# A routing stage in straight code, with four input slots and the matrix products made one and two steps ahead

## What is computed

```
scores = softmax(xf @ gate_w)                        # 8 experts
_, sel = top_k(scores + expert_bias, 2)              # two experts per token
# routed tokens, scaled by their scores, are gathered by expert (sorted by expert number);
# every token also passes the shared expert:
shared = (silu(xf @ sw1) * (xf @ sw3)) @ sw2         # hidden width 224
x = layernorm(x + routed + shared)
```

## Time and profile before

| | us |
|---|---|
| median of 3 runs | 2471.24 |
| lowest and highest | 2467.26, 2482.78 |
| the profiled execution, device time | 2470.14 |
| its span (first to last instruction) | 2468.5 |
| the stage, its start to the start of the next phase | 163.1 |
| granted TensorE clock over the whole span (share of 2.4 GHz) | 0.942 |

### The profile page before, as it was taken

The page is one execution under the profiler, slowest core; times in us unless marked ns, Lnnn a source line. Parts: engine busy times, 40 slices in busy tenths (PEclk is TensorE's granted clock), DMA queues, the critical chain, the costliest instruction groups (busy, mean ns, idle before and its releaser), DMA issues. The chain is left out here.

```text
span 2468.5 us, 60390 instructions
## 1 busy us (share of the span) xinstructions
PE 2021.4 (82%) x19761; PEld 1508.3 (61%) x19761; DVE 1871.6 (76%) x4879; ACT 1552.7 (63%) x2923; POOL 1541.1 (62%) x2367
## 2 busy tenths in 40 slices
PE   8965888888788888888887599888499967878998
PEld 5643655556556556656555488766355535658997
DVE  4546999999999999999999544456433328976886
ACT  5657999999999999999998122255222212333443
POOL 2346888998888999899999323234211125635666
PEclk9986999999999999999999699988699989998999
DMA  5776677766776767676765458544322224531111
GB/s 166 240 219 162 180 188 186 179 185 183 182 191 181 184 183 178 180 195 180 191 183 148 115 161 243 166 143 149 97 81 84 85 75 141 152 94 60 51 56 38
DMA packets 295157, 373.66 MB, mean 151 GB/s; under 512 B 44628, under 2 KB 234647, under 8 KB 294903
## 3 DMA queue, kind: packets, MB, share of 16 engines
q1 hardware_dynamic: 284710, 342.05, 50.2%
q0 software_dynamic: 9872, 27.28, 3.5%
q10 hardware_dynamic: 320, 1.05, 0.2%
HBM read 151.03 MB, written 85.00 MB: 96 GB/s over the span
## 5 line engine op out<-in xcount | busy, mean ns | idle before, releaser
L760 PE MATMUL p_ps_sc<-p_CR,p_BR 64*128 64x128 f32 x4096 | 310.6, 292 | 149.7 <-DVE p_M L1061 91.0
L674 POOL TENSOR_TENSOR p_CR<-p_pc 128x256 f32<-128x256 f32 x512 | 375.2, 733 | 65.3 <-DVE p_pc L1044 52.8
L678 POOL TENSOR_TENSOR p_BR<-p_pb 128x256 f32<-128x256 f32 x512 | 375.2, 733 | 31.0 <-DVE p_pb L1053 13.4
L760 PEld LDWEIGHTS p_ps_sc<-p_CR,p_BR 64*128 64x128 f32 x4096 | 265.2, 194 | 207.3 <-issue 149.9
L906 ACT ACTIVATE p_D<-p_ps_x 128x512 f32<-128x512 f32 x512 | 289.4, 592 | 71.4 <-PE p_ps_x L726 70.0
L1061 DVE TENSOR_TENSOR p_M<-p_ps_sc,p_D 128x1024 f32<-128x1024 f32 x256 | 309.7, 1210 | 6.5 <-issue 3.5
L1044 DVE SCALAR_TENSOR_TENSOR p_pc<-p_ps_c,p_beta,p_cs 128x256 f32<-128x256 f32 x512 | 241.6, 472 | 34.8 <-DMA p_sn<-p_tr_s 17.3
L775 PE MATMUL p_ps_y<-p_M,p_uexp 128*32 128x128 f32 x4096 | 259.8, 282 | 0.0
L1044 DVE SCALAR_TENSOR_TENSOR p_pc<-p_ps_c,p_beta,p_sn 128x256 f32<-128x256 f32 x512 | 241.2, 471 | 0.0
L1053 DVE SCALAR_TENSOR_TENSOR p_pb<-p_ps_b,p_beta,p_cs 128x256 f32<-128x256 f32 x512 | 241.2, 471 | 0.0
L1053 DVE SCALAR_TENSOR_TENSOR p_pb<-p_ps_b,p_beta,p_sn 128x256 f32<-128x256 f32 x512 | 241.2, 471 | 0.0
(11 more groups left out here) (285 smaller groups left out, 5096.3 us busy)
## 6 DMA issues: line engine op xcount, KB each, us to landing
p_cs<-p_tr_c SPq DMA_DIRECT2D x256, 256.0 KB
p_sn<-p_tr_s SPq DMA_DIRECT2D x252, 256.0 KB
p_phib<-scratch_phi SPq DMA_DIRECT2D x256, 128.0 KB
p_x<-scratch_rt SPq DMA_DIRECT2D x72, 128.0 KB, 2.0
scratch_ro<-p_o POOLq DMA_DIRECT2D x72, 128.0 KB, 2.0
p_xT<-in_xT SPq DMA_DIRECT2D x64, 128.0 KB, 4.3
scratch_u<-p_u SPq DMA_DIRECT2D x16, 512.0 KB, 3.6
scratch_wu<-p_wu SPq DMA_DIRECT2D x16, 512.0 KB, 4.3
```

Source lines behind the costliest of these rows:

```text
L674: e.tensor_tensor(CR[:, p, g, :], pc[:, g % 2, 0, :], pc[:, g % 2, 1, :], ALU.add).then_inc(S["rotC"], 1)
L678: e.tensor_tensor(BR[:, p, g, :], pb[:, g % 2, 0, :], pb[:, g % 2, 1, :], ALU.add).then_inc(S["rotB"], 1)
L760: m = e.matmul(sc_ps[half][:, (g * 2 + b) * L:(g * 2 + b + 1) * L], BR[half * 64:half * 64 + 64, p, 2 * q + g, b * L:(b + 1) * L], CR[half ...
```

## The change

The stage is rewritten in its order, in its buffers and in its form; no instruction of the computation itself is added or removed.

- Slots: x1 and x1T have four slots (NX) in place of two, with a semaphore for each slot and tensor. SP's first loads fill four slots; in the steps it does `store(t)`, then `load(t+4)`, x1T before x1. x1T waits only for `b_mm` (steps t and before), x1 for `xr_ok` and `rows_ok`.
- PE: g_ps, a_ps and b_ps exist twice (8 banks in all in place of 5). `gate` runs two steps ahead and `up` one: gate(0), gate(1), up(0), then per step up(t+1), gate(t+2), rank(t), down(t).
- ACT: silu(t), scale_rows(t-1), gate(t+1).
- DVE: choose(t), gate(t+1), finish(t-1), gated(t), place(t).
- All `Fori` loops of the stage are gone on all engines; the 16 steps stand one behind the other, and all waits are against constants.

```diff
-        x1 = sb("x1", [P, 2, BATCH, DM])
-        x1T = sb("x1T", [P, 2, KT, CT])
+        x1 = sb("x1", [P, NX, BATCH, DM])
+        x1T = sb("x1T", [P, NX, KT, CT])
...
-        g_ps, pos_ps = ps("g"), ps("pos")
-        a_ps, b_ps, o_ps = ps("a"), ps("b"), ps("o")
+        pos_ps, o_ps = ps("pos"), ps("o")
+        g_ps, a_ps, b_ps = ([ps(f"{n}{i}") for i in range(2)] for n in "gab")
...
-            def load(t, p):
-                at_least(e, S["xr_ok"], t, 1, -1)
-                at_least(e, S["rows_ok"], t, 4, -4)
-                at_least(e, S["b_mm"], t, 1, -1)
-                e.dma_start(x1[:, p, :, :], tokens_of(W["x1"], t)).then_inc(S["x_in"][p], 16)
-                e.dma_start(x1T[:, p, :, :], turned_of(W["x1T"], t)).then_inc(S["x_in"][p], 16)
+            def load(t):
+                i = t % NX
+                at_least(e, S["b_mm"], t, 1, 1 - NX)
+                e.dma_start(x1T[:, i, :, :], turned_of(W["x1T"], t)).then_inc(xT_in[i], 16)
+                at_least(e, S["xr_ok"], t, 1, 1 - NX)
+                at_least(e, S["rows_ok"], t, 4, 4 - 4 * NX)
+                e.dma_start(x1[:, i, :, :], tokens_of(W["x1"], t)).then_inc(x_in[i], 16)
...
-            stream(e, load, store)
+            for t in range(NX):
+                load(t)
+            for t in range(NC):
+                store(t, t % 2)
+                if t + NX < NC:
+                    load(t + NX)
...
-            two_step_loop(e, step, NC)
+            for t in range(NC):
+                step(t, t % 2)
...
+            gate(0)
+            gate(1)
+            up(0)
+            for t in range(NC):
+                if t + 1 < NC:
+                    up(t + 1)
+                if t + 2 < NC:
+                    gate(t + 2)
                 rank(t)
                 down(t)
...
+            gate(0)
+            for t in range(NC):
+                gated(t)
+                if t:
+                    scale_rows(t - 1, 1 - t % 2)
+                if t + 1 < NC:
                     gate(t + 1)
+            scale_rows(NC - 1, 1)
...
+            gate(0, 0)
+            for t in range(NC):
+                p = t % 2
                 choose(t, p)
+                if t + 1 < NC:
+                    gate(t + 1, 1 - p)
+                if t:
+                    finish(t - 1, 1 - p)
                 gated(t, p)
                 place(t, p)
+            finish(NC - 1, 1)
```

More of the change, by code:

```diff
@@ L1545, in route_and_share @@
         F = Phase(nc, ctx, held, "p3", "prep tri_ok zero_out gate_mm gmax_ok gexp_ok gsum_ok score_ok sb_ok top_ok topi_ok topf_ok eq_ok both_ok "
-                  "acc_ok pos_mm pos_ok pick_ok slot_ok rows_ok a_mm b_mm silu_ok h_ok o_mm xr_ok cnt_mm tab_ok tab_out", "x_in stored sent")
+                  "acc_ok pos_mm pos_ok pick_ok slot_ok rows_ok a_mm b_mm silu_ok h_ok o_mm xr_ok cnt_mm tab_ok tab_out", "stored sent")
         S, sb, ps = F.S, F.sb, F.ps
+        x_in, xT_in = ([signal(nc, held, f"p3_{n}{i}") for i in range(NX)] for n in ("x_in", "xT_in"))
         K, const_in = W["k3"], W["k3_in"]
@@ L1647, in rank, with up @@
                          ).then_inc(S["pos_mm"], 1)
-            def up(t, p):
-                at_least(e, S["h_ok"], t, 1, 0)
-                for w, out, done in ((w1, a_ps, "a_mm"), (w3, b_ps, "b_mm")):
+            def up(t):
+                at_least(e, S["h_ok"], t, 1, -1)
+                for w, out, done in ((w1, a_ps[t % 2], "a_mm"), (w3, b_ps[t % 2], "b_mm")):
                     for hh in range(2):
@@ L1654, in up @@
                             m = e.matmul(out[0:HH, hh * CT:(hh + 1) * CT], w[:, k, hh * HH:(hh + 1) * HH],
-                                         x1T[:, p, k, :], start=(k == 0), stop=(k == KT - 1))
+                                         x1T[:, t % NX, k, :], start=(k == 0), stop=(k == KT - 1))
                     m.then_inc(S[done], 1)
@@ L1693, in scale_rows @@
             def scale_rows(t, p):
-                at_least(e, S["x_in"][p], t - p, 16, 32)
+                e.wait_ge(x_in[t % NX], 16 * (t // NX) + 16)
                 at_least(e, S["slot_ok"], t, 1, 1)
@@ L1699, in scale_rows, with gated @@
                     for n in range(2):
-                        e.activation(rows[:, p, b, n, :], x1[:, p, b, :], ACT.Copy, scale=wts[:, p, b, n:n + 1]).then_inc(S["rows_ok"], 1)
-            def step(t, p, last=False):
+                        e.activation(rows[:, p, b, n, :], x1[:, t % NX, b, :], ACT.Copy, scale=wts[:, p, b, n:n + 1]).then_inc(S["rows_ok"], 1)
+            def gated(t):
                 at_least(e, S["a_mm"], t, 1, 1)
                 at_least(e, S["h_ok"], t, 1, 0)
-                e.activation(sa[:, :, :].rearrange("p n t -> p (n t)"), a_ps[0:HH, :], ACT.Silu).then_inc(S["silu_ok"], 1)
-                scale_rows(t, p)
-                if not last:
-                    gate(t + 1)
[L1709 to L1716, removed]
+                e.activation(sa[:, :, :].rearrange("p n t -> p (n t)"), a_ps[t % 2][0:HH, :], ACT.Silu).then_inc(S["silu_ok"], 1)
+            gate(0)
[4 more added lines that the diff above has]
+                if t + 1 < NC:
+                    gate(t + 1)
+            scale_rows(NC - 1, 1)
         @block.vector
@@ L1796, in finish @@
                     at_least(e, S["stored"][p], t - p, 16, 0)
-                e.tensor_tensor(xr[:, p, :, :], o_ps[:, :].rearrange("p (b d) -> p b d", b=BATCH), x1[:, p, :, :], ALU.add
+                e.tensor_tensor(xr[:, p, :, :], o_ps[:, :].rearrange("p (b d) -> p b d", b=BATCH), x1[:, t % NX, :, :], ALU.add
                                 ).then_inc(S["xr_ok"], 1)
-            def step(t, p, last=False):
+            gate(0, 0)
+            for t in range(NC):
+                p = t % 2
                 choose(t, p)
+                if t + 1 < NC:
+                    gate(t + 1, 1 - p)
+                if t:
+                    finish(t - 1, 1 - p)
                 gated(t, p)
                 place(t, p)
[L1804 to L1814, removed]
+            finish(NC - 1, 1)
             made = S["tab_ok"]
```

28 lines of the change are left out of this document (8 added, 20 removed).

## The result

The changed kernel takes 2456.46 us (median of 9 runs, 2445.95 to 2461.23), the kernel before 2476.69 us in the same series (9 runs, 2467.26 to 2484.67). The ratio is 0.9908, with a 95% interval of 0.9887 to 0.9929. So it is faster, by 0.9%: 20 to 23 us where 34.8 were forecast, and its time lies 3.5 us above the range. Three later series of the same kernel gave 0.9870 [0.9822, 0.9918], 0.9901 [0.9886, 0.9916] and 0.9905 [0.9882, 0.9928]; their medians, 2445.26, 2450.00 and 2450.26 us, lie inside the stated range, in its upper half, and all are above the 2436.4 forecast.

A forecast was written before the change was run, and what follows sets the result against it. A chain of handovers between ACT and DVE was taken to set the 9.07 us step; at 6.5 us a step and a later start the gain was 34.8 us, from 2470.14 to 2435.3, median 2436.4 us, range 2430 to 2453.

The forecast's parts named there:

- another 0.27 brings its result to DVE: Handover from PE's rank to DVE's place: 0.17 us and a handover, 0.27 us in all, within the 6.47 us step.
- if place waits over 0.5 us for rank in each step: Sign at DVE's place instruction that would show the prediction wrong: waiting over 0.5 us for rank in each step.
- Hidden: POOL's four row writes a step, 5.1 us, fit under 6.5 us, unless one write takes over 1.6 us.
- PE's own length: PE's up, gate, rank and down take 6.40 us a step; tied to DVE's loop this gave 6.47, taken as 6.5.
- DVE's own step: DVE's choose, gate, finish, gated and place sum to 6.27 us a step; bounds 5.56 busy alone, 6.48 with the idle bracket.
- load its table right behind the exponentials: ACT's order in a step: silu table until 1.3 us, exponentials until 5.5, hidden with 0.8 us to spare.
- Loads: Loads of x1T for step t+4 land 1.1 us before their gate, so hidden; the loads allow 5.7 us a step.
- Start: Stage start: clock rises about 1614.7, first slots at 1622.9, 4.4 us later than before, 3 us either way.
- The clock: PE's granted clock in the stage: full clock taken, since 6.4 of 6.5 us a step are filled.
- Clock rival: Short PE stops lower the clock: at 0.83 the step is 7.7 us, 2454 us; chance 0.10 mild, 0.04 slower kernel.
- Transfers: Rival: denser DMA traffic stretches the loads; 9.3 us until x1T is at hand gives 8.0 a step, 2459 us; chance 0.08.
- No effect: Rival: exponentials of t+1 still come after place(t), gain under 1%; chance 0.03.

The follow-up runs named there:

- send_late: Changed kernel with the row writes of the first eight steps issued after those of the last eight; first steps 6.12 to 6.14 us, last seven a mean of 6.66.
- send_split: Changed kernel with one more GpSimd wait: the third and fourth row write of step t-1 wait for rank of t; 6.56 us a step, 2443.27 us, ratio 0.9873.
- sa2: Changed kernel with a second tile for sa alone, so silu and its table load don't wait for the last h; 6.92 us a step, ratio 0.9876.
- half_up: Changed kernel with half of up's work left out, four fp32 products a step instead of eight; 6.39 us a step, 2430.95 us (1 run).
- slots_only: Kernel before with only the four input slots, their semaphores and the loops written out, old engine orders kept; 8.54 us a step, ratio 0.9971.
- after_third: Changed kernel unchanged, measured again on chip C; 7.14 us a step, 2450.00 us, ratio 0.9901.
- sa2_rank_mid: Changed kernel with gate and rank moved ahead of up's b-part and a second tile for sa, chip B; 6.08 us a step, 2438.76 us, ratio 0.9847.
- rank_mid: Changed kernel with gate(t+2) and rank(t) moved between the a-part and b-part of up(t+1) on TensorE; 6.54 us a step, ratio 0.989.
- both plain kernels on chip C: Changed kernel, first eight steps' row writes held back, ordinary DMAs from GpSimd or SyncE there instead; 6.12 to 6.25 us a step in the first half.
- both_third: Changed kernel with gate and rank ahead of up's b-part and a second tile for sa, chip C; 7.60 us a step, 2454.54 us, ratio 0.9907.
- pool_work: send_late with four GpSimd additions of 128x256 zeros in each of the first eight steps, chip B; 6.38 us a step, first eight 6.50 to 6.73.
- plain_sp: send_late with extra ordinary writes of the row tiles issued by SyncE in the first eight steps, chip B; 6.12 us a step.

## Why the prediction was wrong

The direction was right, and so was what the new order does to the handovers between ACT and DVE; the size was off by 15 us. Against its own sum: slots from first to last 109.0 us instead of 15 * 6.5 - 0.63 = 96.9 (12.1 us), first slots 19.1 us after the first load instead of 17.0 (2.1 us), the tail 15.2 instead of 14.5 (0.8 us). That is 15.0 us, and the stage brought 19.9 instead of 34.8.

- **The step that failed** is in PE's paragraph: "another 0.27 brings its result to DVE". That has DVE take up the product 0.10 us after rank's end; in ten of the 16 steps it came 0.9 to 3.3 us after it. In steps with no indirect writes 6.13 us a step were measured, and 15 of them take 92 us, so the late landings, with the falls of the clock that followed them, cost 109 - 92 = 17 us in the profiled execution (an estimate from these rows). The prediction had named the sign itself, "if place waits over 0.5 us for rank in each step": it waited 1.36 us a step. The prediction looked at POOL only for whether its four writes fit into a step ("Hidden"), and they do. It didn't ask what runs beside them. The kernel before shows the writes over before rank comes (the first two of four start at 1692.38 and 1693.65, rank at 1699.18 in its timeline), so it had no price for the full meeting. But a small one was there to be seen: in five of its 15 recorded steps the product landed 0.06 to 0.29 us late, each 0.95 to 1.05 us after the end of the last write, and one b product landed 1.19 us late.
- **PE's own length** was 6.40 us from the earlier trace rows and measured 6.13. The step taken there had 2.81 us from the b products to rank, where a step of send_late has 2.54 (1630.76 to 1633.30). The coupled step of 6.47 was therefore 0.34 us longer than what PE alone needs. This error went the other way and hid 5 us of the first.
- **DVE's own step**, 6.27 us by the sum, is at most 5.79: such steps, without a wait of DVE, stand in the profiles of all kernels with the new order and late landings but send_split. The bracket of 0.31 us went with the loop, and its low bound of 5.56 was the nearer one.
- **ACT** was said to load its table right behind the exponentials. It can't: the wait for h stands ahead of the load (10.5 us in 14 steps). The term was wrong and cost nothing, since sa2 without that wait ran no faster than the changed kernel beside it (6.92 against 6.77 us a step).
- **Loads** as predicted in the steps: x1T made two gates wait, both in the start, 7.2 us in all. The slack is small, though: in half_up, whose PE asks sooner, gates waited 7.1 us for x1T. slots_only says what this part is worth together with the unrolled loops, 0.53 us a step.
- **Start.** Up(0) ran at 1.2 GHz nearly throughout (1619.92 to 1626.0). The level rose at about 1624.8, 12.5 us into the stage, where the sum had 8.8. Four executions put the first slots 18.9 to 19.4 us behind the first load.
- **The clock.** Full clock was assumed, 0.95 was measured. It fell for 3 to 4 us three times between the first and the last slots; the first:

```profile
1664.00:1666.00 2.00, 0.50 (x3) 0.40 (x4) 1.93 (x10) 0.86 (x6) 1.55 (x2) 0.95 0.32 113
1666.00:1668.00 2.00, 2.00 (x6) 1.55 (x6) 1.66 (x14) 1.99 (x4) 0.96 (x1) 0.50 0.96 247
1668.00:1670.00 2.00, 2.00 (x8) 1.58 (x7) 1.66 (x13) 1.98 (x4) 0.96 (x1) 0.70 0.82 227
```

  PE was busy 0.50 of the 2 us ahead, because h was late behind a late place, and then the level went from 2.4 to 1.2 GHz. Not every such pause was followed by a fall: in after_third PE was busy 0.28 of 2 us from 1684 on, and the level stayed at 2.4 GHz. So the Clock rival came true in small, as a consequence. Its own cause isn't needed: sa2_rank_mid took the same three pairs of banks in turn on chip B with PE busy 88.65 of 91.3 us and a clock of 1.00. The rule of the Trainium skill named in the prediction (TensorE: Matmul & The Clock Gate, section A second HAM failure mode: psum-queue depth-cycling) is borne out for the idling and not for the cycling. What the half clock costs by itself wasn't separated: steps of 9.0 us are found without it, in after_third.
- **Transfers** and **No effect** played no part that these runs show.
- The profiled execution gained 11.5 us only, since its stage began 6.4 us later than before and the phases behind it took 2 us more. In the three other executions of this kernel the stage began at 1602.7 to 1605.8 (1605.8 before), so this is scatter ahead of the stage and not the change.

What stays open: why a chip holds products back, and what is held, the product in PSUM or the raising of the semaphore that tells of it. That VectorE's raises for results in SBUF were late as well speaks for the raising, without showing it. Every run here is recorded, so whether the recording takes part is open too. The trace of every execution with late landings lacks part of its semaphore records (43,900 to 44,900 are left, against 46,500 to 47,000 in the four of chip B), but so do those of the kernel before (44,288) and of slots_only (44,504), whose products land within 0.3 us. As far as seen, loss of records goes with the chip; lateness needs the indirect writes beside rank, or just ended, too.

## What to carry to other kernels

A closer overlap makes pairs of instructions meet that never met before; for each wait that is left on the path, list what every engine and queue will be doing when it ends, not only whether the hidden work fits. If the trace of before has no such meeting, the handover has no price in it, and the range should say so; if it has it now and then, as here, the rare late case is the one to read. Measure on more than one chip before a step time is taken for the program's: the same kernel, rank_mid with the second tile for sa, had steps of 6.08 us on one and 6.90 and 7.60 us on two others.

## What the runs showed of the hardware that was not expected

- On two of three chips the product of a small TensorE step (rank) mostly lands late, by up to 3.3 us after its recorded end, when GpSimd's indirect writes run across that end or have ended under 1 us before (122 of 139 recorded, against none of 52 without such a write; the first series, whose chip isn't on record, is among them). In send_split they land about 1.1 us after the write's end. Ordinary DMAs of the same tiles, from GpSimd's or SyncE's queue, don't do it (the first nine products of both plain kernels on chip C landed within 0.02 us). Now and then VectorE's own raises are late as well, by up to 1.0 us in both_third.
- GpSimd's arithmetic holds VectorE back in certain instructions. In pool_work, with four additions of 128x256 a step on GpSimd, against plain_sp on the same chip (line, operation, count, busy us and mean ns, idle before):

```profile
L1768 DVE TENSOR_SCALAR p_eq<-k_iota,p_topf 128x8 f32<-128x8 f32 x28 | 7.0, 314 | 0.2
L1771 DVE TENSOR_TENSOR p_both<-p_eq 128x16 bf16<-128x16 f32 x7 | 3.3, 469 | 0.2
```

```profile
L1766 DVE TENSOR_SCALAR p_eq<-k_iota,p_topf 128x8 f32<-128x8 f32 x28 | 4.4, 226 | 0.2
L1769 DVE TENSOR_TENSOR p_both<-p_eq 128x16 bf16<-128x16 f32 x7 | 1.2, 175 | 0.2
```

  The instruction that makes `both` takes 469 ns instead of 175, and most steps 6.55 to 6.57 us instead of 6.12 to 6.17. The Trainium skill (SBUF — State Buffer, section SBUF: two separate sides) has VectorE instructions with two inputs in SBUF and GpSimd instructions that read SBUF lock each other out; this pair agrees. eq and the cast that makes topf (283 ns instead of 175) take one tensor each and grew longer too; this was not looked into further. The Trainium skill also says there that TensorE waits for no other engine's port, so by that rule the late landings are not a matter of ports; no run here tests it.
